# Edge pass of a GNN + FFN kernel: small norm chains on GpSimd, segment marks from memory, a fifth row-made chunk

## Chip, cores and metric

The kernel runs on one core of one Trainium2 chip. The metric is the device time of one execution in microseconds, lower is better. TensorE (PE), VectorE (DVE), ScalarE (ACT), GpSimd (POOL) and SyncE (SP) each work through their own instruction queue in order; what one needs of another it waits for by a semaphore.

## What is computed

A graph layer over 50,000 nodes of 768 features (12 heads of 64) and 25,000 edges sorted by target, then a feed-forward layer. The part that the change touches, cut from the reference:

```python
hv  = layernorm(x).reshape(n, 12, 64)
ft  = einsum('nhd,od->nho', hv, W)
a1  = sum(ft * attn_l, -1);  a2 = sum(ft * attn_r, -1)
e   = leaky_relu(a1[src] + a2[dst], 0.2)
m   = segment_max(e, dst);   w = exp(e - m[dst])
alpha = w / segment_sum(w, dst)[dst]
agg = segment_sum(alpha * ft[src], dst)
out = relu(agg + einsum('nhd,od->nho', hv, W_res))
```

After it `x + out` goes through a second layernorm and `gelu(. @ W1 + b1) @ W2 + b2`, in a node pass of 392 tiles that the change leaves alone.

## The kernel before

**Tiling.** The edge pass takes the edges in 196 chunks of 128 (one edge per partition). Seven chunks are a group (`G`, 28 groups); fourteen are a body (`BODY`), the unit of the loop `turns(...)` that each engine runs for itself. An engine's turn `c` does the stages of different chunks: a stage with lag `L` works on chunk `c - L`. GpSimd runs some five turns ahead of VectorE: its power for a group's target norms stands at turn 7g+23 of its own loop (L604 to L610), where VectorE's use of it stands at turn 7g+18 (L1348 to L1362).

**GpSimd** (L602 to L653). Per chunk: the gather of source rows (L619), the gather of target rows through `gather_targets` (L597) and a scatter of row numbers to `row_scratch` (L638), each an indirect DMA behind a `settle` (a no-op that keeps its place). Per group: two powers to the minus one half over seven columns, `r_d` for the target norms (L610) and `r_s` for the source norms (L653; L647 for group 0).

**VectorE** (from L1172). Per chunk: `bn_stats`/`bn_aggr` of the gathered source rows (L1105, L1108), the one-hot mask (L1312), the message product `ft * alpha` (L1255, two inputs from SBUF) and the sum row with its mean correction (L1237). Per group: the small norm operations `ve_s` (L1190, variance + eps, then GpSimd's power) and `nm_s` (L1202); `ve_d` (L1246), then after GpSimd's power `nmd` (L1354) and the edge scores `e_col` (L1356 to L1362); `same_x` (L1183), the marks "same target as the edge before" spread over heads; the copies of the transposed scores and marks `e_row`, `same_r` (L1318, L1319); `pen_r` (L1367); four scans (L1369 to L1385); softmax factors (L1325 to L1329).

**Target scores** are made in two ways. In ten of fourteen chunks PE transposes the target rows too and takes the products (L910, L947, L973), and VectorE copies 13 columns (L1219). In the four chunks of `OFF_PE` they are row-made: ScalarE takes the mean of the target rows (L763), VectorE multiplies them by a row of weights (L1345) and reduces per head (L1336). ScalarE also normalizes the source rows with `nm_s` and `r_s` (L742) and squares the target rows with an accumulator into `q_d` (L787).

**PE** per group transposes `e_col` and `same_x` into one bank (L934, L935), and later the weights and totals (L940, L941). **SP** loads the targets of a group over all partitions (L512) and stores each chunk's sum row to `agg_scratch` (L518), in the order of its loop.

```python
w = (i - 7) // G % 2
dve.wait_ge(s_ag, G * (gv + 1))
V.tensor_scalar(ve_s[:, w, :], mvs[:, w, :, 1], EPS, None, ALU.add).then_inc(s_ve, 1)
```

```python
pool.wait_ge(s_ved, gd + 1)
settle(pool)
pool.tensor_tensor(r_d[:, w, :], ve_d[:, w, :], half[:, 0:G], ALU.pow).then_inc(s_rpd, 1)
```

Of the kernel before, what the change touches and what calls it, by code (L numbers as in the profile page):

```python
# [8 lines left out]
D = 768  # L9
HEADS = 12  # L10
# [4 lines left out]
P = 128  # L15
# [11 lines left out]
G = 7  # L27
# [32 lines left out]
OFF_PE = (1, 6, 8, 13)  # L60
# [76 lines left out]
def gnn_ffn_kernel(nc, x, x_cols, edges, dst_rows, dst_next, dst_prev, dst_ends, chunk_base, sel_heads,  # L137
# [9 lines left out]
    with ExitStack() as ctx:  # L147
# [8 lines left out]
        row_d = nc.dram_tensor("row_scratch", [NP, RW], i32).ap()  # L156
        cls_d = nc.dram_tensor("cls_scratch", [NCLS, D], f32).ap()
# [88 lines left out]
        same_x = sb("same_x", [P, 2, HG])  # L246
# [85 lines left out]
        cnt_ps = ps[0:EH, 5, 0:2]  # L332
        a2_ps = ps[:, 6, 2 * P:2 * P + HM]
# [32 lines left out]
        s_dsl = sem("s_dsl")  # L366
# [101 lines left out]
        def _(sp):  # L468
# [12 lines left out]

            sp.dma_start(ident[:], eye).then_inc(l_const, 16)
# [110 lines left out]
        def _(pool):  # L593
# [4 lines left out]

            pool.wait_ge(l_edges, 16 * 3)
            for b in turns(pool, NB, 2):  # L600
                for i in range(BODY):
# [43 lines left out]
                    if isinstance(b, int) and c == G + 1:  # L645
                        pool.wait_ge(s_ve, 1)
                        pool.tensor_tensor(r_s[:, 0, :], ve_s[:, 0, :], half[:, 0:G], ALU.pow).then_inc(s_rp, 1)  # L647
                    gp = 2 * b + (i - 11) // G
                    if k == 11 % G and exists(gp, NG) and not (isinstance(gp, int) and gp == 0):
                        w = (i - 11) // G % 2  # L650
                        pool.wait_ge(s_ve, gp + 1)
                        settle(pool)
                        pool.tensor_tensor(r_s[:, w, :], ve_s[:, w, :], half[:, 0:G], ALU.pow).then_inc(s_rp, 1)  # L653
# [74 lines left out]
        def _(act):  # L728
# [5 lines left out]
            for b in turns(act, NB, 2):  # L734
                for i in range(BODY):
# [14 lines left out]
                    if exists(ct, EC):  # L750
# [5 lines left out]
                        if (i - L_TR) % BODY in OFF_PE:  # L756
# [822 lines left out]
```

## Time and profile before

| | us |
|---|---|
| median of three runs | 2668.76 (2667.09 to 2670.31) |
| profiled execution: its time | 2669.66 |
| its span, first to last instruction | 2667.8 |
| busy: PE, VectorE, ScalarE, GpSimd | 2562.7, 2472.9, 2364.0, 2142.9 |
| edge pass, about | 0 to 950 |
| node pass, about | 1000 to 2650 |

A row of instruction groups gives line, engine, operation, output and inputs with shapes, the number of instructions, their busy time, the mean of one in ns, and the idle time of the engine just in front of them with what ended it. "issue" means that the profile shows nothing that the engine waited for. A timeline row gives start, duration and, in brackets, idle time in front. Matmul ends are modelled, and spans on GpSimd are rough.

### The profile page before, as it was taken

What the parts mean: (1) busy time and instruction counts of PE and PEld (TensorE: products, weight loads), DVE (VectorE), ACT (ScalarE), POOL (GpSimd) and SP (SyncE); (2) the same over time, 40 slices, a digit from 0 to 9 for tenths busy, and PEclk for the clock granted to TensorE, in tenths of its full rate; (3) what the DMA queues carried; (4) which work ended last, traced back from release to release, by engine and by line L of the source; (5) the groups of instructions that cost most, each with busy time, mean ns of one, the idle gap of its engine ahead of it and who ended that gap; (6) DMA issues with size and microseconds to landing.
All of it is one profiled execution on the core that took longest, in us unless ns stands there. A gap on an engine that the chain in (4) does not pass through costs nothing. (4 is left out here: it accounts for less than half of the span.)

```text
span 2667.8 us, 67341 instructions
## 1 busy us (share of the span) xinstructions
PE 2562.7 (96%) x20334; PEld 2315.5 (87%) x20334; DVE 2472.9 (93%) x4949; ACT 2364.0 (89%) x4748; POOL 2142.9 (80%) x2029
## 2 busy tenths in 40 slices
PE   5899999999999967999999999999999999999998
PEld 4777777777777846999999999999999999999997
DVE  6799999999999886999999999999999999999996
ACT  4999999999999955999999999999999999999993
POOL 6777777877777618888888888888888888888882
PEclk9999999999999987999999999999999999999999
DMA  8788888878888567999999999999999999999983
GB/s 313 225 268 268 266 267 264 271 265 265 265 269 266 172 210 276 353 345 336 333 333 326 323 326 324 321 319 316 310 326 316 316 318 314 313 310 311 313 311 120
DMA packets 254176, 777.85 MB, mean 292 GB/s; under 512 B 77185, under 2 KB 85165, under 8 KB 253837
## 3 DMA queue, kind: packets, MB, share of 16 engines
q1 hardware_dynamic: 184190, 563.88, 59.7%
q0 software_dynamic: 69312, 210.37, 25.5%
q8 instruction: 121, 1.98, 0.3%
q14 instruction: 121, 0.99, 0.1%
q10 hardware_dynamic: 432, 0.62, 0.1%
HBM read 638.86 MB, written 236.65 MB: 328 GB/s over the span
## 5 line engine op out<-in xcount | busy, mean ns | idle before, releaser
L1057 PE MATMUL ps<-wr_bd,arena 128*128 128x128 f32 x4704 | 593.9, 277 | 13.9 <-DVE arena L1457 13.9
L1057 PEld LDWEIGHTS ps<-wr_bd,arena 128*128 128x128 f32 x4704 | 563.8, 193 | 15.3 <-issue 15.2
L723 POOL DMA_INDIRECT arena<-agg_scratch,nrow x392 | 439.1, 1120 | 77.7 <-issue 66.0
L664 POOL TENSOR_SCALAR arena<-csr_neg,mv,r_n 128x768 f32<-128x768 f32 x392 | 387.2, 988 | 51.1 <-PE ps L893 37.9
L1452 DVE SCALAR_TENSOR_TENSOR ps<-ps,r_n,arena 128x768 f32<-128x768 f32 x392 | 399.1, 1018 | 12.5 <-DMA arena<-agg_scratch,nrow 10.8
L843 ACT ACTIVATE t_hi<-ps 128x768 fp32r<-128x768 f32 x392 | 314.5, 802 | 93.9 <-PE ps L893 93.8
L1457 DVE SCALAR_TENSOR_TENSOR arena<-ps,arena 128x768 f32<-128x768 f32 x392 | 375.5, 958 | 13.4
L852 ACT ACTIVATE arena<-arena,s_st 128x768 f32<-128x768 f32 x392 | 363.8, 928 | 25.0 <-DVE arena L1457 25.0
L713 POOL TENSOR_SCALAR arena<-arena,nm_n,r_n 128x768 f32<-128x768 f32 x392 | 383.2, 978 | 2.5 <-issue 1.7
L1464 DVE TENSOR_TENSOR t_lo<-ps,t_hi 128x768 fp32r<-128x768 f32 x392 | 373.6, 953 | 12.6 <-ACT t_hi L843 12.4
L811 ACT ACTIVATE arena<-arena,mv 128x768 f32<-128x768 f32 x392 | 367.8, 938 | 12.8
L1440 DVE TENSOR_TENSOR arena<-arena,ps 128x768 f32<-128x768 f32 x392 | 369.9, 944 | 6.8 <-PE ps L1048 6.6
L1032 PE MATMUL ps<-t_hi,w_hi 128*96 128x256 f32 x1176 | 362.1, 308 | 0.0
L1032 PE MATMUL ps<-t_hi,w_lo 128*96 128x256 f32 x1176 | 330.6, 281 | 0.0
L893 PE MATMUL ps<-ident,arena 128*128 128x128 f32 x2352 | 323.3, 274 | 7.2 <-POOL arena L713 6.5
L1032 PE MATMUL ps<-t_lo,w_hi 128*96 128x256 f32 x1176 | 329.8, 280 | 0.0
L804 ACT ACTIVATE arena<-arena 128x768 f32<-128x768 f32 x392 | 326.2, 832 | 2.6 <-DMA nrow<-row_scratch 1.9
L658 POOL TENSOR_TENSOR r_n<-ve_n,half 128x4 f32<-128x4 f32 x200 | 208.3, 1041 | 119.1 <-DVE ve_n L1162 118.3
L919 PE MATMUL ps<-wgv,arena 128*128 128x130 f32 x2352 | 299.1, 277 | 0.0
L919 PEld LDWEIGHTS ps<-wgv,arena 128*128 128x128 f32 x2352 | 282.1, 193 | 0.2 <-issue 0.2
L893 PEld LDWEIGHTS ps<-ident,arena 128*128 128x128 f32 x2352 | 270.7, 142 | 9.0 <-POOL arena L713 8.2
L910 PE MATMUL ps<-ident,arena 128*128 128x128 f32 x2016 | 260.4, 277 | 16.1 <-DVE arena L1223 13.4
(226 smaller groups left out, 6171.5 us busy)
## 6 DMA issues: line engine op xcount, KB each, us to landing
arena<-in_x SPq DMA_DIRECT2D x196, 768.0 KB
arena<-in_x_cols SPq DMA_DIRECT2D x392, 384.0 KB, 5.2
out<-arena SPq DMA_DIRECT2D x195, 768.0 KB, 5.7
agg_scratch<-agg_ring SPq DMA_DIRECT2D x196, 384.0 KB, 3.6
dst_all<-in_dst_rows SPq DMA_DIRECT2D x28, 256.0 KB
arena<-agg_scratch,nrow POOLq DMA_INDIRECT x392
arena<-in_x,e_slot POOLq DMA_INDIRECT x364, 4.8
dst_all<-in_dst_rows SPq DMA_DIRECT2D x28, 192.0 KB
```

The lines of the kernel that those rows point to most:

```text
L664: pool.tensor_scalar(g_ring[:, g, :].rearrange("p (c f) -> p c f", f=P), csr_neg[:, None, :].to_broadcast([P, NC, P]), mv1[:, w, 2 * (v % ...
L713: pool.tensor_scalar(n2[:, v % 2, :], y_ring[:, v, :], nm_n[:, w, k:k + 1], r_n[:, w, PAIR + k:PAIR + k + 1], ALU.add, ALU.mult).then_inc( ...
L723: pool.indirect_dma_start(g_ring[:, g, :], None, agg_d, bass.IndirectOffsetOnAxis(nrow[:, v, 3:4], 0), bounds_check=EP - 1, oob_is_err=Fal ...
L811: nc.scalar.activation(junk[:, 0, :], x_ring[:, v, :], ACT.Square, bias=mv1[:, w, 2 * k:2 * k + 1], scale=-1.0, accum_out=q_st[:, w, k:k + ...
L893: last = nc.tensor.transpose(dst[:, c * P:(c + 1) * P], src[:, c * P:(c + 1) * P], ident[:])
L919: last = nc.tensor.matmul(ft_ps[:, n // 3, n % 3, :], both_t[:, v, n * P:(n + 1) * P], wgv[:, n, :], start=True, stop=True)
L1032: last = nc.tensor.matmul(ps[0:HID, 6 + v, 0:PAIR * P], w[:, i, :], h[:, i, :], start=(i == 0 and n == 0), stop=(i == NC - 1 and n == 2))
L1057: last = nc.tensor.matmul(res_ps(b, tr)[:, i * P:(i + 1) * P], xt_ring[:, g, i * P:(i + 1) * P], wr_bd[:], start=True, stop=True)
L1440: V.tensor_tensor(y_ring[:, v, :], y_ring[:, v, :], down_ps(b, to), ALU.add).then_inc(s_o, 1)
L1452: V.scalar_tensor_tensor(z, z, r_n[:, w, k:k + 1], g_ring[:, g, :], ALU.mult, ALU.add).then_inc(s_z1, 1)
L1457: V.scalar_tensor_tensor(y_ring[:, v, :], z, 0.0, x_ring[:, v, :], ALU.max, ALU.add, accum_out=s_st[:, w5, k:k + 1]).then_inc(s_y, 1)
L1464: V.tensor_tensor(t2_lo[:, v, :, f], pair(0).rearrange("p (c n) -> p c n", c=NC), t2_hi[:, v, :, f].bitcast(f32), ALU.subtract).then_inc(s ...
```

## The change

1. Five small operations per group move from VectorE to GpSimd, around the powers there: `ve_s`, the negated mean and its product with `r_s` (one VectorE operation before, two on GpSimd), `ve_d` and `nmd`. GpSimd now waits for `s_ag` and `s_sqd` itself, and each dependent step within a chain waits for the step before.
2. The segment marks are transposed once by PE (turn 12), kept as `same` and `(same - 1) * BIG`, written by SP to a scratch tensor with one copy per head, and loaded by SP per group straight into `same_r` and `pen_r`. `same_x`, its transpose, the copy of `same_r` and the operation for `pen_r` go.
3. `OFF_PE` gets a fifth member, 11.

```diff
-OFF_PE = (1, 6, 8, 13)
+OFF_PE = (1, 6, 8, 11, 13)
+        seg_d = nc.dram_tensor("seg_scratch", [2, EC, HEADS, P], f32).ap()
+        seg_t = agg_ring[0:EH, 2, 0:4 * P].rearrange("p (k n e) -> p k n e", k=2, n=2)
+        seg_ps = ps[0:EH, 5, 2 * P:4 * P].rearrange("p (n e) -> p n e", n=2)
...
+            def load_segments(g):
+                for k, rows in enumerate((same_r, pen_r)):
+                    sp.dma_start(rows[:, 0:P], seg_d[k].rearrange("(g c) h e -> g (c h) e", c=G)[ds(g, 1)].rearrange("g r e -> (g r) e"))                        .then_inc(d_seg, 16)
...
+                    if isinstance(b, int) and b == 1 and i == 0:
+                        sp.wait_ge(s_idx, 2)
+                        for k in range(2):
+                            for n in range(2):
+                                sp.dma_start(seg_d[k, n * EH:(n + 1) * EH], seg_t[:, k, n, :][:, None, :].to_broadcast([EH, HEADS, P]))                                    .then_inc(d_seg, 16)
+                        sp.wait_ge(d_seg, 16 * 4)
+                        load_segments(0)
+                    gs_ = 2 * b + (i - 21) // G + 1
+                    if (i - 21) % G == 0 and exists(gs_, NG) and not (isinstance(gs_, int) and gs_ < 1):
+                        sp.wait_ge(s_tot, gs_)
+                        load_segments(gs_)
...
+            def source_scale(w, gp):
+                pool.wait_ge(s_ag, G * (gp + 1))
+                at_least(pool, s_norm, G * (gp - 1))
+                settle(pool)
+                pool.tensor_scalar(ve_s[:, w, :], mvs[:, w, :, 1], EPS, None, ALU.add).then_inc(s_ve, 1)
+                pool.tensor_scalar(nm_s[:, w, :], mvs[:, w, :, 0], -1.0, None, ALU.mult).then_inc(s_ve, 1)
+                pool.wait_ge(s_ve, 2 * gp + 2)
+                settle(pool)
+                pool.tensor_tensor(r_s[:, w, :], ve_s[:, w, :], half[:, 0:G], ALU.pow).then_inc(s_rp, 1)
+                pool.wait_ge(s_rp, gp + 1)
+                settle(pool)
+                pool.tensor_tensor(nm_s[:, w, :], nm_s[:, w, :], r_s[:, w, :], ALU.mult).then_inc(s_nm, 1)
...
+                        pool.wait_ge(s_sqd, G * (gd + 1))
+                        settle(pool)
+                        pool.tensor_scalar(ve_d[:, w, :], q_d[:, w, :], 1.0 / D, EPS, ALU.mult, ALU.add).then_inc(s_ved, 1)
                         pool.wait_ge(s_ved, gd + 1)
+                        at_least(pool, s_e, 2 * (gd - 1))
                         settle(pool)
                         pool.tensor_tensor(r_d[:, w, :], ve_d[:, w, :], half[:, 0:G], ALU.pow).then_inc(s_rpd, 1)
+                        pool.wait_ge(s_rpd, gd + 1)
+                        at_least(pool, s_eo, G * (gd - 1))
+                        settle(pool)
+                        pool.tensor_tensor(nmd[:, w, :], a2_all[:, w, :, HEADS], r_d[:, w, :], ALU.mult).then_inc(s_nmd, 1)
...
-                        pool.tensor_tensor(r_s[:, 0, :], ve_s[:, 0, :], half[:, 0:G], ALU.pow).then_inc(s_rp, 1)
+                        source_scale(0, 0)
...
+                            at_least(act, s_nmd, 2 * b + (i - L_TR) // G - 1)
...
-                        nc.tensor.transpose(row_ps[:, 0:P], e_col[:, w, :], ident[:])
-                        nc.tensor.transpose(row_ps[:, P:2 * P], same_x[:, w, :], ident[:]).then_inc(s_ert, 1)
+                        nc.tensor.transpose(row_ps[:, 0:P], e_col[:, w, :], ident[:]).then_inc(s_ert, 1)
...
+                        for n in range(2):
+                            nc.tensor.transpose(seg_ps[:, n, :], same_f[:, n * EH:(n + 1) * EH], ident[:])
...
-                        V.tensor_copy(same_x[:, w, :].rearrange("p (g h) -> p g h", h=HEADS),
-                                      same_f[:, ds(G * gc, G)][:, :, None].to_broadcast([P, G, HEADS])).then_inc(s_dsl, 1)
...
-                        V.tensor_scalar(ve_s[:, w, :], mvs[:, w, :, 1], EPS, None, ALU.add).then_inc(s_ve, 1)
...
-                        V.scalar_tensor_tensor(nm_s[:, w, :], mvs[:, w, :, 0], -1.0, r_s[:, w, :],
-                                               ALU.mult, ALU.mult).then_inc(s_nm, 1)
...
-                        V.tensor_scalar(ve_d[:, w, :], q_d[:, w, :], 1.0 / D, EPS, ALU.mult, ALU.add).then_inc(s_ved, 1)
...
+                        V.tensor_copy(seg_t[:, 0], seg_ps)
+                        V.tensor_scalar(seg_t[:, 1], seg_ps, 1.0, BIG, ALU.subtract, ALU.mult).then_inc(s_idx, 1)
...
+                        if k == 0:
+                            at_least(dve, s_nm, 2 * b + i // G - 1)
                         source_stats(c, i, i // G, k, 2 * b + i // G)
...
-                        V.tensor_copy(same_r[:, 0:P], row_ps[:, P:2 * P]).then_inc(s_same, 1)
...
-                        V.tensor_tensor(nmd[:, w, :], a2_all[:, w, :, HEADS], r_d[:, w, :], ALU.mult).then_inc(s_nmd, 1)
...
-                        V.tensor_scalar(pen_r[:, 0:P], same_r[:, 0:P], 1.0, BIG, ALU.subtract, ALU.mult).then_inc(s_seg, 1)
-                        dve.wait_ge(s_seg, 3 * gm + 1)
+                        dve.wait_ge(d_seg, 32 * gm + 96)
```

## Rows read from the trace of the kernel before

**Rows 1.** Busy time by stretch; engine busy us (instructions), clock, DMA share, GB/s.

```profile
0.00:100.00 100.00, 61.24 (x504) 55.21 (x505) 59.75 (x180) 63.98 (x118) 71.74 (x74) 0.95 0.79 268
...
200.00:300.00 100.00, 98.22 (x787) 78.39 (x785) 95.83 (x227) 91.00 (x178) 78.79 (x71) 1.00 0.82 268
```

**Rows 2.** Waits of 200 to 800 us: us in total, times, longest.

```profile
ACT arena L742 <- DVE nm_s L1202: 27.4, 18, 1.8
...
DVE nmd L1354 <- POOL r_d L610: 0.5, 3, 0.2
```

**Rows 3.** GpSimd's groups, 162.18 to 818.60 us: busy us, mean ns, idle before, releasers.

```profile
L638 POOL DMA_INDIRECT row_scratch<-e_slot x140 | 157.9, 1128 | 44.5 <-issue 37.4 <-PE ps L910 5.9 <-DVE ve_d L1246 0.9
...
L619 POOL DMA_INDIRECT arena<-in_x,e_slot x140 | 152.4, 1088 | 46.4 <-issue 43.2 <-PE ps L963 2.6 <-ACT arena L787 0.3
...
L610 POOL TENSOR_TENSOR r_d<-ve_d,half 128x7 f32<-128x7 f32 x20 | 40.0, 2000 | 3.0 <-DVE ve_d L1246 3.0
```

**Rows 4.** GpSimd's timeline, five of the `r_d` powers: start us, us, instruction, idle before.

```profile
73.87 1.54 POOL L610 TENSOR_TENSOR r_d<-ve_d,half 128x7 f32<-128x7 f32 x1
...
467.43 1.54 POOL L610 TENSOR_TENSOR r_d<-ve_d,half 128x7 f32<-128x7 f32 x1
...
499.97 1.53 POOL L610 TENSOR_TENSOR r_d<-ve_d,half 128x7 f32<-128x7 f32 x1
...
531.71 2.08 POOL L610 TENSOR_TENSOR r_d<-ve_d,half 128x7 f32<-128x7 f32 x1 [0.16 <-DVE ve_d L1246]
...
893.78 1.55 POOL L610 TENSOR_TENSOR r_d<-ve_d,half 128x7 f32<-128x7 f32 x1
```

**Rows 5.** VectorE's groups, 195.32 to 326.51 us (four groups of chunks).

```profile
L1345 DVE SCALAR_TENSOR_TENSOR arena<-arena,a_all 128x768 f32<-128x768 f32 x8 | 8.1, 1011 | 0.0
...
L1336 DVE TENSOR_REDUCE a_all<-arena 128x12 f32<-128x768 f32 x8 | 7.6, 946 | 0.0
...
L1219 DVE COPY a_all<-ps 128x13 f32<-128x13 f32 x20 | 3.3, 166 | 0.0
...
L1367 DVE TENSOR_SCALAR pen_r<-same_r 84x128 f32<-84x128 f32 x4 | 1.3, 336 | 0.1
...
L1319 DVE COPY same_r<-ps 84x128 f32<-84x128 f32 x4 | 1.1, 272 | 0.0
...
L1183 DVE COPY same_x<-same_f 128x84 f32 x4 | 0.9, 230 | 0.0
...
L1190 DVE TENSOR_SCALAR ve_s<-mvs 128x7 f32<-128x7 f32 x4 | 0.7, 180 | 0.7 <-issue 0.7
...
L1246 DVE TENSOR_SCALAR ve_d<-q_d 128x7 f32<-128x7 f32 x4 | 0.7, 164 | 0.0
...
L1202 DVE SCALAR_TENSOR_TENSOR nm_s<-mvs,r_s 128x7 f32<-128x7 f32 x4 | 0.6, 156 | 0.0
```

**Rows 6.** DMA issues: KB each, median us to landing.

```profile
agg_scratch<-agg_ring SPq DMA_DIRECT2D x196, 384.0 KB, 3.6
```

**Rows 7.** GpSimd in the node pass (timeline) and its memset at the start.

```profile
1499.62 1.04 POOL L658 TENSOR_TENSOR r_n<-ve_n,half 128x4 f32<-128x4 f32 x1 [0.26 <-DVE ve_n L1162]
...
1500.87 0.99 POOL L664 TENSOR_SCALAR arena<-csr_neg,mv,r_n 128x768 f32<-128x768 f32 x1 [0.21 <-PE ps L893]
...
L1569 POOL MEMSET const-float32-1.0<- 128x1 f32 x1 | 0.1, 98 | 0.0
```

**Rows 8.** Timeline of VectorE and GpSimd around 400 us.

```profile
399.98 0.96 DVE L1255 TENSOR_TENSOR arena<-arena,alpha 128x768 f32<-128x768 f32 x1
...
400.24 2.08 POOL L610 TENSOR_TENSOR r_d<-ve_d,half 128x7 f32<-128x7 f32 x1 [0.18 <-DVE ve_d L1246]
```

**Rows 9.** Single lines, 130 to 850 us: duration ns min/median/max, first and last start.

```profile
L619 POOL DMA_INDIRECT arena<-in_x,e_slot x154: 965/1022/1472, 129.7 to 846.6; - x154
...
L638 POOL DMA_INDIRECT row_scratch<-e_slot x154: 1001/1012/1692, 132.3 to 849.4; - x154
...
L1255 DVE TENSOR_TENSOR arena<-arena,alpha x153: 944/952/957, 133.3 to 846.7; 128x768 f32<-128x768 f32 x153
```

More of the change, by code:

```diff
@@ L245, in gnn_ffn_kernel @@
         dst_slot = sb("dst_slot", [P, 2, G])
-        same_x = sb("same_x", [P, 2, HG])
         bn_a = sb("bn_a", [P, 2, 2, 6])
@@ L365, in gnn_ffn_kernel @@
         s_nmd = sem("s_nmd")
-        s_dsl = sem("s_dsl")
+        d_seg = sem("d_seg")
         s_norm = sem("s_norm")
@@ L645, in _ @@
                     if isinstance(b, int) and c == G + 1:
-                        pool.wait_ge(s_ve, 1)
-                        pool.tensor_tensor(r_s[:, 0, :], ve_s[:, 0, :], half[:, 0:G], ALU.pow).then_inc(s_rp, 1)
+                        source_scale(0, 0)
                     gp = 2 * b + (i - 11) // G
                     if k == 11 % G and exists(gp, NG) and not (isinstance(gp, int) and gp == 0):
[L650 to L653, printed above, removed]
+                        source_scale((i - 11) // G % 2, gp)
             def power(w, q):
@@ L1179, in _ @@
                         w = (i - 17) // G % 2
-                        at_least(dve, s_ert, gc - 1)
                         at_least(dve, s_mask, G * (gc - 1))
                         V.tensor_copy(dst_slot[:, w, :], dstbf[:, ds(G * gc, G)])
-                        V.tensor_copy(same_x[:, w, :].rearrange("p (g h) -> p g h", h=HEADS),
-                                      same_f[:, ds(G * gc, G)][:, :, None].to_broadcast([P, G, HEADS])).then_inc(s_dsl, 1)
                     gv = 2 * b + (i - 7) // G
                     if k == 0 and exists(gv, NG):
-                        w = (i - 7) // G % 2
-                        dve.wait_ge(s_ag, G * (gv + 1))
-                        V.tensor_scalar(ve_s[:, w, :], mvs[:, w, :, 1], EPS, None, ALU.add).then_inc(s_ve, 1)
                         if isinstance(gv, int) and gv == 0:
@@ L1195, in _ @@
                             V.tensor_tensor(w2_lo[:], w2_sb, w2_hi[:].bitcast(f32), ALU.subtract).then_inc(s_wgv, 1)
-                    gn = 2 * b + (i - 8) // G
-                    if k == 1 and exists(gn, NG):
-                        w = (i - 8) // G % 2
-                        dve.wait_ge(s_rp, gn + 1)
-                        at_least(dve, s_norm, G * (gn - 1))
-                        V.scalar_tensor_tensor(nm_s[:, w, :], mvs[:, w, :, 0], -1.0, r_s[:, w, :],
-                                               ALU.mult, ALU.mult).then_inc(s_nm, 1)
                     ge = 2 * b + (i + 6) // G
@@ L1242, in _ @@
                     gd = 2 * b + (i - L_VD) // G
-                    if (i - L_VD) % G == 0 and exists(gd, NG):
-                        w = (i - L_VD) // G % 2
-                        dve.wait_ge(s_sqd, G * (gd + 1))
-                        V.tensor_scalar(ve_d[:, w, :], q_d[:, w, :], 1.0 / D, EPS, ALU.mult, ALU.add).then_inc(s_ved, 1)
                     cm = c - L_MSG
@@ L1317, in _ @@
                             at_least(dve, s_esc, on_pe(b, i - L_FT + 1))
-                        V.tensor_copy(e_row[:], row_ps[:, 0:P])
-                        V.tensor_copy(same_r[:, 0:P], row_ps[:, P:2 * P]).then_inc(s_same, 1)
+                        V.tensor_copy(e_row[:], row_ps[:, 0:P]).then_inc(s_same, 1)
                     if (i - 21) % G == 0 and exists(ga, NG):
@@ L1352, in _ @@
                         dve.wait_ge(s_eft, G * (gd + 1))
-                        at_least(dve, s_eo, G * (gd - 1))
-                        V.tensor_tensor(nmd[:, w, :], a2_all[:, w, :, HEADS], r_d[:, w, :], ALU.mult).then_inc(s_nmd, 1)
                         at_least(dve, s_ert, gd - 1)
@@ L1366, in _ @@
                         dve.wait_ge(s_same, gm + 1)
-                        V.tensor_scalar(pen_r[:, 0:P], same_r[:, 0:P], 1.0, BIG, ALU.subtract, ALU.mult).then_inc(s_seg, 1)
-                        dve.wait_ge(s_seg, 3 * gm + 1)
+                        dve.wait_ge(d_seg, 32 * gm + 96)
                         V.tensor_tensor_scan(f_row[:], pen_r[:, 0:P], e_row[:], -BIG, ALU.add, ALU.max)\
                             .then_inc(s_seg, 1)
-                        dve.wait_ge(s_seg, 3 * gm + 2)
+                        dve.wait_ge(s_seg, 2 * gm + 1)
                         at_least(dve, s_wst, gm)
@@ L1374, in _ @@
                                              ALU.add, ALU.max).then_inc(s_seg, 1)
-                        dve.wait_ge(s_seg, 3 * gm + 3)
+                        dve.wait_ge(s_seg, 2 * gm + 2)
                         V.tensor_tensor(f_row[:], e_row[:], m_row[:], ALU.subtract).then_inc(s_z, 1)
```

1 line of the change is left out of this document (removed).

## The prediction

> **What bounds the kernel now.** The change touches only the edge pass, so I read that stretch alone. The busy table first: from 200 to 300 us PE, VectorE and ScalarE stand at 98, 96 and 91% and GpSimd at 79% [rows 1]. By shares GpSimd has room; the next views say otherwise. The table of waits (200 to 800 us, 18 groups of seven chunks): VectorE waits 0.5 us for GpSimd's `r_d` and, elsewhere, for nothing but its own results; ScalarE waits 27.4 us for VectorE's `nm_s` [rows 2]. So VectorE sets the pace and ScalarE follows. GpSimd's groups come third. Before each of its gathers and scatters it stands about 0.3 us, mostly for no cause that the profile knows ("issue"): 44.5 us before the 140 scatters of L638, 37.4 of it so [rows 3]. Three DMA instructions of about 1 us and three such gaps fill most of a chunk's 4.7 us, and twice in seven chunks a power of 1.5 to 2.1 us comes on top. Beyond that its one regular wait is 3.0 us in 20 groups, 0.15 us each, for VectorE's `ve_d` [rows 3].
>
> How much room is that? The order of the powers in time tells. At 467.43 and 499.97 us `r_d` started with no idle time in front of it (GpSimd was late), and the next began at 531.71 with 0.16 us of waiting. Those two groups took GpSimd 32.54 and 31.58 us, on average 32.06 [rows 4]. From the first `r_d` (73.87) to the 26th (893.78), 25 groups took 819.91 us, 32.80 each [rows 4]. GpSimd thus has about 0.74 us to spare in a group, and VectorE waits for `r_d` in that same group: there is no deeper buffer between the two.
>
> **VectorE, what goes.** Per group: `same_x` 0.230, `same_r` 0.272, `pen_r` 0.336, and four operations on seven columns (`ve_s`, `nm_s`, `ve_d`, `nmd`) between 0.156 and 0.180, together 0.66; 0.18 of idle time before `ve_s` goes too: 1.68 us [rows 5]. What comes: a fifth row-made chunk in fourteen, 1.011 + 0.946 for product and reduction, less a copy of 0.166: 1.79 us per body, 0.90 per group [rows 5]. Net 0.78 us less per group: VectorE alone would take 32.02.
>
> **PE, ScalarE, SP.** PE loses six transposes, six score products and one small product per body and a transpose per group; VectorE does not wait for PE, so I count nothing. ScalarE trades three copies and a score copy for two copies and one 768-column pass with an accumulator; whatever the difference, 1.5 us per group of standing before `nm_s` covers it [rows 2]; without that cover it would lie on the path at full price. SP gets two loads of 42 KB per group behind `s_tot`. That count comes from VectorE's turn 7g+13, and the store queued behind it waits for turn 7g+14, so the wait delays nothing; scans use the marks five chunks (23 us) later, while a 384 KB store lands in 3.6 us [rows 6]. Cover gone, its landing time would stand before the first scan. Four writes of 588 KB at the start take about 9 us at 268 GB/s [rows 1]; behind them in SP's queue is the first target load, five turns later. Two transposes and two small PSUM operations there fall into a stretch in which VectorE is 60% busy [rows 1]: nothing. The new waits of VectorE (`s_nm`, two groups old) and ScalarE (`s_nmd`, likewise) are long met.
>
> **GpSimd, what comes.** Per group five operations on seven columns: `ve_s`, the negated mean and the product with `r_s`, and `ve_d` and `nmd`. All three gathers or scatters of a chunk stand behind them, and behind `r_d` VectorE's `e_col`. In front of them are waits for `s_ag` and `s_sqd`; the operations that waited for these on VectorE stood 0.18 us without a named cause (`ve_s`) and not at all (`ve_d`) [rows 5], and GpSimd comes later than VectorE did: zero. The trace has no such operation. From below: a memset of one column, 0.10 us, which reads nothing [rows 7]. From above: the four-column power, 1.04 [rows 7], of which much is the power itself. Between: seven columns take 1.54 [rows 4], four 1.04, so 0.167 per column and about 0.37 for none. These operations read SBUF as that power does, so I take 0.30, an estimate, near that value. Each chain gains two dependent steps within GpSimd; in the node pass the operation that follows its power so starts 0.21 us after it [rows 7]. Sum: 5 x 0.30 + 4 x 0.21 = 2.34 us.
>
> **A lock, by row and rule.** `r_d` at 400.24 took 2.08 instead of 1.54 us; it started 0.26 us into VectorE's message product (399.98 to 400.94) [rows 8]. The gathers show the same in their spread, 965 to 1472 ns, while the 153 message products lie between 944 and 957 [rows 9]: GpSimd pays, VectorE never. The Trainium skill, SBUF — State Buffer, section on the two sides of SBUF, says a VectorE instruction with two SBUF inputs and a GpSimd instruction that reads SBUF exclude each other, whichever starts first. The trace agrees for GpSimd as the second and not for VectorE as the second; were that half to hold, ten short operations per body would also hold VectorE up, by my estimate well under 1 us per body. The lock now costs about 2.2 us per group (seven source gathers and seven scatters at means of 1088 and 1128 against least values of 965 and 1001 ns, and 0.46 for `r_d`) [rows 3, 9], over nine such passes of VectorE (seven message products, two products of row-made chunks). The fifth row-made chunk is half a product more per group: 0.12 us.
>
> **Sum.** GpSimd: 32.06 + 2.34 + 0.12 = 34.52 us per group against VectorE's 32.02. GpSimd becomes the bound: it waits for nobody, and VectorE stands before `e_col`. 25 groups x 34.52 = 863.0, which is 43.1 more than 819.91. Before the first `r_d`, for which VectorE already waited, three more chains: about 3 us. After the 26th VectorE paces again and gains about 2 us in the last two groups. Together +44 on the profiled execution's 2669.66: 2713.8; that execution is 0.9 above the median of the runs, so 2713.
>
> The Trainium skill, GPSIMD Engine Reference, section Performance versus the Vector engine, gives 4497 ns for 2048 columns; at that rate seven cost 0.015 us (an estimate from that page) and the sum would be some 38 us lower, 2675.
>
> **Rivals.** (a) GpSimd keeps up and VectorE paces: 25 x 0.78 = 20 us less, 2649. Its place is GpSimd's queue between two `r_d`. It needs 34.52 to fall to 32.02: operations at 0.10 give back 1.0, and the lock would have to give back another 1.5 of its 2.2, which it can, since where GpSimd's starts fall depends on phase. For it: one late group took GpSimd only 31.58 [rows 4]. Against it: two losses must shrink together. It decides where GpSimd's group passes 32.02. (b) Nothing to see: operations at 0.10 and a lock cost smaller by 0.7: 32.8 per group, 2670. (c) Operations at the price of the four-column power, 1.04: 3.7 us more in each of 25 groups and 6 in the first chains, 2811. (d) The marks arrive late and each scan waits: 3.6 us on 28 groups would be 100 us, but only if the loads were queued five chunks late; nothing in SP's order does that.
>
> **Chances.** The forecast, GpSimd pacing with operations between 0.10 and 0.38: 0.72, and its own range is 2686 (0.10) to 2735 (0.38 and a lock 0.45 per group dearer). (a) 0.16, (b) 0.08, (c) and (d) together 0.04. The range holds (b) and much between (a) and (b): 2655 to 2745. What a measurement of this kernel can tell from no change is about 0.2% (5 us; the runs before span 3.2). Faster 0.16, within it 0.08, slower 0.76.
>
> **Signs.** Right, if `r_d` stand about 34.5 us apart, GpSimd shows no idle time before them, VectorE stands about 2.5 us per group before `e_col` with `r_d` as releaser, and the five operations measure 0.2 to 0.4. Wrong, if the powers again wait for VectorE or ScalarE (then (a)), if the small operations are far from 0.30, or if VectorE stands before the scans (then (d)). One more message-product stretch should show in GpSimd's mean durations.

## The result and the profile after

The changed kernel takes 2744.13 us (median of four runs, 2741.94 to 2746.37) against 2669.53 us before (four runs, 2667.09 to 2673.12): ratio 1.0278 [1.0261, 1.0296], slower by 74.6 us. 44 us were forecast (2713), and the measured median lies 1 us inside the upper end of the range, 2745. The profiled execution of after took 2742.53 us with a span of 2740.7, 72.9 more than the span before.

**Where the time went.** GpSimd's timeline of after, four of its `r_d` powers (start us, us, instruction, idle before):

```profile
76.60 1.51 POOL L644 TENSOR_TENSOR r_d<-ve_d,half 128x7 f32<-128x7 f32 x1
...
361.00 1.52 POOL L644 TENSOR_TENSOR r_d<-ve_d,half 128x7 f32<-128x7 f32 x1 [0.24 <-POOL ve_d L640]
...
397.61 1.52 POOL L644 TENSOR_TENSOR r_d<-ve_d,half 128x7 f32<-128x7 f32 x1 [0.23 <-POOL ve_d L640]
...
966.12 1.52 POOL L644 TENSOR_TENSOR r_d<-ve_d,half 128x7 f32<-128x7 f32 x1 [0.17 <-POOL ve_d L640]
```

The first and the 26th stand 889.52 us apart, 35.58 per group (36.6 and 34.5 in turn for most of the way), where [rows 4] gave 819.91 and 32.80: +69.6 us. The first `r_d` comes 2.7 later. From the 26th to the end it takes 1774.6 us, against 1774.0 before. 2.7 + 69.6 + 0.6 = 72.9, the whole difference of the spans: all of it arises in the steady groups of the edge pass and in the start.

**Who paces.** The busy table of after, 200 to 300 us (columns as in [rows 1]):

```profile
200.00:300.00 100.00, 89.78 (x689) 70.95 (x681) 87.81 (x188) 85.61 (x165) 76.96 (x79) 0.98 0.79 246
```

VectorE's groups of after, 200 to 860 us (columns as in [rows 5]):

```profile
L1373 DVE TENSOR_TENSOR e_col<-a_all,r_d 128x84 f32<-128x84 f32 x18 | 4.6, 258 | 49.7 <-ACT arena L809 30.6 <-POOL r_d L644 19.1
```

Against [rows 1] PE, VectorE and ScalarE lost 8, 8 and 5 points of busy share, and GpSimd 2: its busy share does not show that it now paces. VectorE stands 49.7 us in 18 groups, 2.76 each, before `e_col`, where it had waited 0.5 us in all for GpSimd before [rows 2]. The row puts 30.6 us of this on a ScalarE copy, and here it misleads, as the timelines of VectorE and ScalarE around 399 us show:

```profile
398.40 0.83 ACT L809 ACTIVATE arena<-ps 128x780 f32<-128x780 f32 x1
...
399.35 0.25 DVE L1373 TENSOR_TENSOR e_col<-a_all,r_d 128x84 f32<-128x84 f32 x1 [3.40 <-ACT arena L809]
```

`r_d` of that group ran from 397.61 to 399.13, and `e_col` began 0.22 us later. The copy named belongs to another chunk; the last one that `e_col` needs had ended at 386.87, 12 us before. In every group of this stretch `e_col` begins 0.22 to 0.23 us after its `r_d` has ended, so all 49.7 us are waits for GpSimd.

GpSimd's groups of after, 200 to 860 us (busy us, mean ns, idle before, releasers), to set beside [rows 3]:

```profile
L657 POOL DMA_INDIRECT arena<-in_x,e_slot x130 | 151.5, 1165 | 52.1 <-issue 39.7 <-PE ps L945 9.1 <-ACT arena L822 2.4
L676 POOL DMA_INDIRECT row_scratch<-e_slot x130 | 143.3, 1102 | 39.6 <-issue 34.1 <-PE ps L996 4.3 <-ACT arena L822 0.6
L614 POOL DMA_INDIRECT arena<-in_x,e_slot x130 | 135.6, 1043 | 41.1 <-issue 36.9 <-PE ps L996 2.4 <-ACT arena L776 1.8
L644 POOL TENSOR_TENSOR r_d<-ve_d,half 128x7 f32<-128x7 f32 x19 | 28.9, 1520 | 4.4 <-POOL ve_d L640 4.4
L624 POOL TENSOR_TENSOR r_s<-ve_s,half 128x7 f32<-128x7 f32 x18 | 27.4, 1520 | 2.7
L620 POOL TENSOR_SCALAR ve_s<-mvs 128x7 f32<-128x7 f32 x18 | 5.7, 317 | 0.4
L648 POOL TENSOR_TENSOR nmd<-a_all,r_d 128x7 f32<-128x7 f32 x18 | 5.3, 292 | 4.0 <-POOL r_d L644 4.0
L621 POOL TENSOR_SCALAR nm_s<-mvs 128x7 f32<-128x7 f32 x18 | 4.5, 252 | 1.4
L640 POOL TENSOR_SCALAR ve_d<-q_d 128x7 f32<-128x7 f32 x19 | 4.1, 216 | 1.4
L627 POOL TENSOR_TENSOR nm_s<-nm_s,r_s 128x7 f32<-128x7 f32 x19 | 4.1, 216 | 2.7
```

L657 is the source gather (L619 before), L676 the scatter (L638), L614 the target gather (L597). The five new operations take 216 to 317 ns, 1.28 us per group together. The powers now wait only for GpSimd's own step in front of them. GpSimd works through its list without a stop for VectorE, and that list has become the group's time.

**The account of a group.** From such rows I take a group of each kernel apart (200 to 860 us). *Stretch* is what the three DMA instructions take beyond their least durations, 7 times the sum of (mean less least), with 965, 942 and 1001 ns as least for source gather, target gather and scatter: here 7 x (200 + 101 + 101) = 2.81 us. *Powers* is what the two powers take beyond 1.512 us each, *idle* is the idle time before all of GpSimd's instructions, *small* the operations of the chains. *Group* is 7 x 660 us over the number of chunks counted in the stretch, so it is good to some 0.25 us; the spacing of the `r_d` is the finer measure:

| us per group | group | stretch | powers | idle | small |
|---|---|---|---|---|---|
| before | 32.77 | 1.95 | 0.54 | 6.98 | 0 |
| after | 35.54 | 2.81 | 0.02 | 8.07 | 1.28 |

+0.86, -0.52, +1.09 and +1.28 make 2.71 of the 2.77 that the group grew. GpSimd's timeline of after shows the idle part, in both chains:

```profile
411.98 0.31 POOL L620 TENSOR_SCALAR ve_s<-mvs 128x7 f32<-128x7 f32 x1
412.37 0.25 POOL L621 TENSOR_SCALAR nm_s<-mvs 128x7 f32<-128x7 f32 x1
412.78 1.52 POOL L624 TENSOR_TENSOR r_s<-ve_s,half 128x7 f32<-128x7 f32 x1
414.44 0.21 POOL L627 TENSOR_TENSOR nm_s<-nm_s,r_s 128x7 f32<-128x7 f32 x1
415.34 1.11 POOL L657 DMA_INDIRECT arena<-in_x,e_slot  x1 [0.69 <-issue]
...
431.64 0.21 POOL L640 TENSOR_SCALAR ve_d<-q_d 128x7 f32<-128x7 f32 x1
432.09 1.52 POOL L644 TENSOR_TENSOR r_d<-ve_d,half 128x7 f32<-128x7 f32 x1 [0.24 <-POOL ve_d L640]
433.83 0.21 POOL L648 TENSOR_TENSOR nmd<-a_all,r_d 128x7 f32<-128x7 f32 x1 [0.22 <-POOL r_d L644]
434.73 1.08 POOL L657 DMA_INDIRECT arena<-in_x,e_slot  x1 [0.69 <-issue]
```

Each dependent step costs 0.2 us, as forecast. What was not: the gather behind a short operation starts 0.58 to 0.69 us after its end; behind a power, in the kernel before, it was nearly always 0.18 to 0.20. In both cases that is twice in a group.

### The profile page after: what moved, and what is told of

Same layout as the page of the kernel before. It is cut to its first block and busy times, and to the rows that moved or that the text cites. A ratio compares the mean times of both kernels' runs of the same rounds, so it can differ in the third digit from the quotient of the medians.

```text
span 2740.7 us, 66968 instructions
## 1 busy us (share of the span) xinstructions
PE 2550.6 (93%) x20028; PEld 2299.2 (84%) x20028; DVE 2471.8 (90%) x4769; ACT 2368.3 (86%) x4748; POOL 2190.5 (80%) x2169
## 5 line engine op out<-in xcount | busy, mean ns | idle before, releaser
L928 PE MATMUL ps<-ident,arena 128*128 128x128 f32 x2352 | 321.9, 273 | 7.6 <-POOL arena L747 6.8
L776 ACT ACTIVATE arena<-arena,nm_s,r_s 128x768 f32<-128x768 f32 x196 | 200.4, 1023 | 83.6 <-POOL nm_s L627 83.6
```

What stands on the lines that cost most here:

```text
L928: last = nc.tensor.transpose(dst[:, c * P:(c + 1) * P], src[:, c * P:(c + 1) * P], ident[:])
```

## The experiments

Each kernel was timed against the kernel before on the same chip (its medians there 2670.7 to 2671.5 us). Theory 1 is the prediction's: GpSimd's list of work sets the group, and the chains and the lock lengthen it. The lock is what the prediction calls it: VectorE's passes with two SBUF operands (the message product and the product of a row-made chunk) hold GpSimd's instructions up.

**Four row-made chunks instead of five**, with chains and marks as in after:

```diff
-OFF_PE = (1, 6, 8, 11, 13)
+OFF_PE = (1, 6, 8, 13)
```

> The changed kernel with four row-made chunks again, chains on GpSimd and marks from memory kept. Theory (GpSimd's instruction stream paces the edge pass, 35.5 us per group): only 0.12 us of stalls per group go, 2741 us (2733 to 2746), and VectorE stands longer before e_col. Rival 1 (VectorE paces; what was added to it is what costs): 0.90 us per group in 28 groups, 2719. Rival 2 (the marks from memory are what costs): no change, 2744, but then chains_dve stays high as well.

Measured: 2716.49, 1.0176 [1.0159, 1.0193]. A miss: one chunk in fourteen is worth 27.6 us, not a few. GpSimd's three DMA lines, 200 to 860 us:

```profile
L614 POOL DMA_INDIRECT arena<-in_x,e_slot x134 | 143.4, 1070 | 42.3 <-issue 31.4 <-ACT arena L776 5.8 <-PE ps L996 5.1
L657 POOL DMA_INDIRECT arena<-in_x,e_slot x134 | 141.4, 1055 | 54.2 <-issue 40.7 <-PE ps L945 11.1 <-ACT arena L822 2.4
L676 POOL DMA_INDIRECT row_scratch<-e_slot x134 | 138.9, 1037 | 40.8 <-issue 34.1 <-PE ps L996 5.8 <-PE ps L945 0.6
```

Stretch falls from 2.81 to 7 x (90 + 128 + 36) = 1.78 us; idle (8.08) and small operations (1.27) stay. The group falls by 0.97 (35.58 to 34.61 by the spacing of the `r_d`), so it is stretch alone. The time also lies near rival 1's 2719, but VectorE does not pace here. It still stands 2.1 us per group for `r_d`, as its table of waits shows (us in total, times, longest):

```profile
DVE e_col L1373 <- POOL r_d L644: 40.1, 19, 3.4
```

Half a product per group lasts 0.5 us and can hold GpSimd no longer than that by itself; where the rest comes from is counted below, behind the run without the message product.

**Both chains back on VectorE**, five chunks and marks kept:

```diff
-            def source_scale(w, gp):
...
-                        source_scale((i - 11) // G % 2, gp)
+                        w = (i - 11) // G % 2
+                        pool.wait_ge(s_ve, gp + 1)
+                        settle(pool)
+                        pool.tensor_tensor(r_s[:, w, :], ve_s[:, w, :], half[:, 0:G], ALU.pow).then_inc(s_rp, 1)
...
-                        pool.tensor_scalar(ve_d[:, w, :], q_d[:, w, :], 1.0 / D, EPS, ALU.mult, ALU.add).then_inc(s_ved, 1)
...
+                        V.tensor_scalar(ve_s[:, w, :], mvs[:, w, :, 1], EPS, None, ALU.add).then_inc(s_ve, 1)
...
+                        V.scalar_tensor_tensor(nm_s[:, w, :], mvs[:, w, :, 0], -1.0, r_s[:, w, :],
+                                               ALU.mult, ALU.mult).then_inc(s_nm, 1)
...
+                        V.tensor_scalar(ve_d[:, w, :], q_d[:, w, :], 1.0 / D, EPS, ALU.mult, ALU.add).then_inc(s_ved, 1)
...
+                        V.tensor_tensor(nmd[:, w, :], a2_all[:, w, :, HEADS], r_d[:, w, :], ALU.mult).then_inc(s_nmd, 1)
```

> The changed kernel with both small chains back on VectorE (as before the change), five row-made chunks and marks from memory kept. Theory: GpSimd is back at about 32.2 us per group and VectorE paces with 32.80 - 0.84 + 0.90 = 32.86: 2671 us (2666 to 2680). Rival 1 (the fifth row-made chunk costs): about 2694 or more. Rival 2 (marks from memory cost): stays above 2700.

Measured: 2677.13, 1.0025 [1.0012, 1.0037]. As expected; rivals 1 and 2 fall. The chains on GpSimd are worth 67.0 of the 74.6 us (2744.13 - 2677.13).

**Only one of the chains on GpSimd.** The edit above for the target chain alone (the source chain stays on GpSimd):

```diff
-                        pool.tensor_scalar(ve_d[:, w, :], q_d[:, w, :], 1.0 / D, EPS, ALU.mult, ALU.add).then_inc(s_ved, 1)
...
-                        pool.tensor_tensor(nmd[:, w, :], a2_all[:, w, :, HEADS], r_d[:, w, :], ALU.mult).then_inc(s_nmd, 1)
...
+                        V.tensor_scalar(ve_d[:, w, :], q_d[:, w, :], 1.0 / D, EPS, ALU.mult, ALU.add).then_inc(s_ved, 1)
```

> Only the source chain (s_ag, ve_s, mean, r_s, nm_s) on GpSimd; the target chain back on VectorE; five row-made chunks and marks kept. Theory: about half of what both chains add to GpSimd's 32.2 us per group, 0.79 for three operations, 0.4 for two handshakes and 0.45 for the later start of the gather behind the short operation: 33.8 per group, 2669 + 25 x 1.0 = 2695 (2685 to 2710). Rival (the target chain alone does it, as it is the one that VectorE waits for): 2675 or less.

Measured: 2713.99, 1.0167 [1.0150, 1.0184], above the range. And the other way round, the source chain back on VectorE and the target chain left on GpSimd:

```diff
-            def source_scale(w, gp):
...
+                        V.tensor_scalar(ve_s[:, w, :], mvs[:, w, :, 1], EPS, None, ALU.add).then_inc(s_ve, 1)
...
+                        V.scalar_tensor_tensor(nm_s[:, w, :], mvs[:, w, :, 0], -1.0, r_s[:, w, :],
+                                               ALU.mult, ALU.mult).then_inc(s_nm, 1)
```

> Only the target chain (s_sqd, ve_d, r_d, nmd) on GpSimd, the source chain back on VectorE; five row-made chunks and marks kept. Theory: 0.51 for two operations, 0.45 for two handshakes, 0.45 for the later gather, on GpSimd's 33.0 us per group: 34.2, 2703 us (2693 to 2715). Rival (the chains cost only together): 2685 or less.

Measured: 2687.66, 1.0059 [1.0042, 1.0076], below the range and next to the rival. So the target chain alone costs 10.5 us over no chain, the source chain alone 36.9, both 67.0: they don't add up. In the account:

| us per group | group | stretch | powers | idle | small |
|---|---|---|---|---|---|
| no chain on GpSimd | 33.08 | 1.89 | 0.57 | 7.28 | 0 |
| target chain | 33.64 | 2.29 | 0.16 | 7.28 | 0.60 |
| source chain | 34.39 | 2.86 | 0.03 | 7.18 | 1.03 |
| both (after) | 35.54 | 2.81 | 0.02 | 8.07 | 1.28 |

The small operations cost what they take. Stretch and powers change with every shift of GpSimd's starts, by up to 1 us, and only the kernel with both chains pays more idle time.

**The lock, taken away.** The message product reads two operands from SBUF; here two `bn_stats` passes over the same rows, with one operand each, stand in its place. The messages stay unweighted, so the softmax weights don't reach the output:

```diff
-                        V.tensor_tensor(msg, msg,
-                                        per_head(alpha[:, w, j * HEADS:(j + 1) * HEADS])[:, :, :, None]
-                                        .to_broadcast([P, NC, HC, DH]), ALU.mult).then_inc(s_msg, 1)
+                        for h in range(2):
+                            last = V.bn_stats(bn_m[:, v, h, :], ft_ring[:, v, 3 * h:3 * h + 3, :].rearrange("p a b -> p (a b)"))
+                        last.then_inc(s_msg, 1)
```

> The changed kernel without the message product: in its place two bn_stats passes over the same chunk of ft_ring (one SBUF input each, some 0.1 us longer together), so the messages are left unweighted. Theory (VectorE's passes with two SBUF inputs hold GpSimd's instructions up): of 2.8 us of stretched gathers and scatters per group about 2 go, 33.5 us per group, 2744 - 50 = 2694 us (2684 to 2720), gathers close to their least durations although VectorE is busier. Rival (the stretch belongs to the gathers themselves or to any work of VectorE): 2738 or more.

Measured: 2702.13, 1.0120 [1.0100, 1.0140], 42.0 us below after, although VectorE's passes are longer (2 x 553 against 951 ns). GpSimd's DMA lines and VectorE's new passes:

```profile
L658 POOL DMA_INDIRECT arena<-in_x,e_slot x136 | 143.8, 1057 | 54.3 <-issue 45.4 <-PE ps L997 5.8 <-PE ps L946 3.1
L677 POOL DMA_INDIRECT row_scratch<-e_slot x137 | 139.9, 1022 | 41.7 <-issue 35.7 <-PE ps L997 5.5 <-PE ps L946 0.6
L615 POOL DMA_INDIRECT arena<-in_x,e_slot x136 | 136.1, 1001 | 43.0 <-issue 40.7 <-PE ps L997 2.1 <-ACT arena L823 0.3
...
L1272 DVE BATCH_NORM_STATS2 bn_m<-arena 128x6 f32<-128x390 f32 x272 | 139.2, 553 | 0.0
```

Stretch falls to 1.20 us; the group falls by 1.65 (to 33.89), of which stretch is 1.61. 25 x 1.65 = 41 us: the whole gain. So 1.6 of the 2.8 us of stretch go with the message product's second SBUF operand. By itself this run leaves a rival: the new passes also shift the phase, and phase alone changes stretch. The traces close it. In after, VectorE's pass first, then the GpSimd instruction that started while it ran:

```profile
215.25 0.95 DVE L1271 TENSOR_TENSOR arena<-arena,alpha 128x768 f32<-128x768 f32 x1
...
215.44 1.65 POOL L676 DMA_INDIRECT row_scratch<-e_slot  x1 [0.31 <-issue]
...
228.19 1.01 DVE L1364 SCALAR_TENSOR_TENSOR arena<-arena,a_all 128x768 f32<-128x768 f32 x1
...
228.29 1.77 POOL L657 DMA_INDIRECT arena<-in_x,e_slot  x1 [0.30 <-issue]
```

The message product ends at 216.20 and the scatter 0.89 us later; the row-made product ends at 229.20 and the gather 0.86 us later. A held instruction thus ends its least duration, less some 0.1 us, after the pass that it met. Over the traces of the eleven kernels here that have both the message product and GpSimd's powers (200 to 860 us), by where a DMA instruction starts (only those directly behind another DMA instruction; some steps of 0.1 us are left out):

| start, counted from the start of the nearest two-operand pass, us | instructions | mean stretch, us |
|---|---|---|
| 0.8 to 0.2 before | 682 | 0.01 |
| 0.1 before to 0.1 after | 166 | 0.39, from 0 to 0.90 |
| 0.1 to 0.2 after | 72 | 0.70 |
| 0.3 to 0.4 after | 185 | 0.48 |
| 0.5 to 0.6 after | 157 | 0.30 |
| 0.7 to 0.8 after | 83 | 0.09 |
| 0.8 to 0.9 after | 28 | 0.01 |

One pass costs GpSimd between nothing and 0.9 us, by where in it the instruction starts. In after, 102 of 390 instructions end in this way behind a pass; they hold 43.2 of 52.4 us of stretch, 29.4 behind message products (1.58 us per group, as much as went without them) and 13.9 behind row-made products. With four row-made chunks it is 19.9 and 0.2 us, in 72 of 402. What stays without the message product is for the most part, 13.2 of 24.5 us, behind the row-made products. The powers follow the same rule: before, 18 of 21 `r_d` started 0.24 to 0.25 us into a message product and took 2.08 us, as in [rows 8]; in after none does, hence 1.52.

The other side of it, in after (duration ns min/median/max, 130 to 900 us):

```profile
L1271 DVE TENSOR_TENSOR arena<-arena,alpha x151: 944/951/978, 133.3 to 898.4; 128x768 f32<-128x768 f32 x151
```

As before [rows 9], VectorE's product is never longer than its median by more than some 30 ns, now with five more GpSimd operations per group, and VectorE does not stand idle in front of one either (0.0 us in all before the 130 of 200 to 860 us). The Trainium skill, SBUF — State Buffer, section "SBUF: two separate sides", says that whichever of the two starts first holds the shared ports and the other waits for the whole instruction. These runs agree for GpSimd as the one that waits and show nothing of VectorE waiting.

**The same with the marks alone** (messages unweighted, four chunks, chains on VectorE); the edit is the one above and that of the next run together.

> The same replacement in the kernel with the marks alone (which took 2678 us with VectorE waiting for r_d in every group). Theory (there GpSimd paces through these stalls, 3.6 us per group): GpSimd falls to about 31, VectorE paces with 31.96 + 0.5 to 0.9, r_d waits for ve_d again, 2662 us (2652 to 2674). Rival (the marks' loads cost): 2678 or more, up to 2690 as VectorE does more.

Measured: 2718.38, 1.0182 [1.0164, 1.0200], a miss by 56 us, and no test of the lock. Its table of waits, 200 to 860 us:

```profile
DVE ve_s L1205 <- issue: 40.5, 9, 5.2
POOL r_s L671 <- DVE ve_s L1205: 39.4, 16, 4.7
```

Once per body VectorE stands 4 to 5 us at the same place for no cause that the profile names, and GpSimd waits for it. Of its DMA queues the second instruction queue (q14) carried 176 packets here and 120 to 122 in all the others. More instruction packets and the stops come together; that one causes the other isn't shown. What can be read: stretch is 0.89 here, the least of all these kernels.

**Marks alone**, four chunks, chains on VectorE:

```diff
-OFF_PE = (1, 6, 8, 11, 13)
+OFF_PE = (1, 6, 8, 13)
...
+                        V.tensor_scalar(ve_d[:, w, :], q_d[:, w, :], 1.0 / D, EPS, ALU.mult, ALU.add).then_inc(s_ved, 1)
```

> Only the marks from memory: both chains on VectorE, four row-made chunks. Theory: VectorE needs 31.96 us per group and GpSimd, late all the time, 32.06: about 25 x 0.74 us below before, 2651 (2647 to 2658), with r_d starting without idle time in front in many groups. If VectorE alone paced: 2646. Rival 2 (marks from memory cost): no faster than 2669.

Measured: 2678.19, 1.0030 [1.0019, 1.0042]. A miss, and the most telling one: VectorE does 0.84 us less per group (`same_x`, `same_r`, `pen_r` [rows 5]), and the kernel is 7.5 us slower. GpSimd's groups, 200 to 860 us:

```profile
L655 POOL DMA_INDIRECT row_scratch<-e_slot x140 | 182.5, 1304 | 42.7 <-issue 36.6 <-DVE ve_d L1260 3.0 <-PE ps L978 3.0
L614 POOL DMA_INDIRECT arena<-in_x,e_slot x139 | 152.8, 1100 | 42.4 <-issue 33.5 <-PE ps L927 5.8 <-DVE ve_d L1260 3.0
L636 POOL DMA_INDIRECT arena<-in_x,e_slot x139 | 138.3, 995 | 37.8 <-issue 28.0 <-PE ps L978 5.2 <-PE ps L927 4.6
L670 POOL TENSOR_TENSOR r_s<-ve_s,half 128x7 f32<-128x7 f32 x20 | 33.9, 1693 | 0.3
L627 POOL TENSOR_TENSOR r_d<-ve_d,half 128x7 f32<-128x7 f32 x20 | 30.8, 1538 | 0.1
```

VectorE's wait for it, from the table of waits of the same stretch:

```profile
DVE nmd L1369 <- POOL r_d L627: 16.0, 20, 1.4
```

`r_d` no longer waits for `ve_d` (0.1 us in 20 groups; 3.0 before [rows 3]), and VectorE waits for `r_d` in every group: GpSimd paces, at 33.2 us, without a chain on it. Stretch is 7 x (303 + 158 + 30) = 3.44 against 1.95. Against before, a group has 0.8 us less idle time and 0.3 less in the powers, and 1.5 more stretch. In the same count as above, 109 of 417 instructions meet a message product here, 0.56 us each, where before 79 of 422 met a pass, 0.40 us each: the starts have moved to the front of the product. The idle time that I had read as room went into that.

**Fewer row-made chunks**, from marks alone and from the kernel before: fewer two-operand passes, so less stretch by theory 1; the rival was that only the places where the passes fall count.

```diff
-OFF_PE = (1, 6, 8, 13)
+OFF_PE = (1, 6, 11)
```

> The marks from memory, both chains on VectorE, three row-made chunks (1, 6, 11). VectorE would need 31.06 us per group. Theory (GpSimd paces through its stalls; a row-made product less per body takes 0.5 to 1.0 us of them per group off, as between five and four): 32.2 to 32.7 per group against 33.2 with four, 2653 to 2666 us. Rival 1 (PE, with one more chunk of transposed target rows, paces): 2678 or more. Rival 2 (the stalls depend on phase alone): anywhere from 2650 to 2690, without relation to the number of products.

Measured (three chunks, marks): 2688.37, 1.0065 [1.0051, 1.0079].

```diff
-OFF_PE = (1, 6, 8, 13)
+OFF_PE = (1, 8)
```

> As marks3 with two row-made chunks (1, 8). VectorE would need 30.2 us per group. Theory: another 0.5 to 1.0 us of stalls per group off, down to GpSimd's 31.5 to 32: 2640 to 2655. Rival 1 (PE paces): more than marks3. Rival 2 (phase alone): no order between the two.

Measured (two chunks, marks): 2677.60, 1.0027 [1.0018, 1.0036].

```diff
-OFF_PE = (1, 6, 8, 13)
+OFF_PE = (1, 6, 11)
```

> The kernel before with three row-made chunks in place of four and nothing else. VectorE would need 31.9 us per group, as much as in the kernel with marks alone and four. Theory: GpSimd paces, with a product less per body: 32.2 to 33.2 per group, 2655 to 2678 us. If VectorE alone paced: 2646. Rival (PE paces): 2678 or more.

Measured (three chunks, otherwise the kernel before): 2700.53, 1.0113 [1.0098, 1.0129]. Three misses. With marks, five, four, three and two chunks give 2677, 2678, 2688 and 2678 us: no order. But these three times are no test of the lock alone. VectorE's waits, with three and with two chunks and marks (200 to 860 us):

```profile
DVE a_all L1233 <- PE ps L988: 29.9, 38, 1.4
...
DVE a_all L1233 <- PE ps L988: 35.7, 30, 1.4
```

VectorE stands 1.4 to 1.8 us per group for the score products of PE (28.0 us in the kernel with three chunks and no other change), where before and with the marks alone it stands for them not at all, and it waits for `r_d` no more than 3.5 us in all. So rival 1, PE, is in these times, and with three chunks it fits them (2688 and 2701, against 2678 or more). What the three can show is the stretch: 1.65, 3.19 and 1.88 us per group in the order of the runs. The scatter with two chunks and marks, the fewest passes of all:

```profile
L655 POOL DMA_INDIRECT row_scratch<-e_slot x140 | 180.1, 1286 | 42.7 <-issue 33.8 <-DVE ve_d L1260 5.5 <-PE ps L927 3.4
```

It is stretched as in marks alone with four: 89 of 420 instructions meet a pass, 0.63 us each. The number of passes is not what decides. That theory falls, and for the stretch rival 2, phase, stands: what counts is where in a pass an instruction starts.

**One more short operation on GpSimd behind each chain**, its result unused:

```diff
+                pool.tensor_tensor(dup[:, 0, :], half[:, 0:G], r_s[:, w, :], ALU.mult)
...
+                        pool.tensor_tensor(dup[:, 1, :], half[:, 0:G], r_d[:, w, :], ALU.mult)
```

> The changed kernel with one more short GpSimd operation (seven columns, no dependents) behind each chain. In the changed kernel the gather behind a chain starts 0.6 to 0.7 us after the last short operation, where it starts 0.2 us after a power. Theory 1 (a gather needs some 0.9 us from the start of what is in front of it, and a short operation leaves that uncovered): the added operation lies in that gap, 2744 to 2748. Theory 2 (each operation costs its own length): 0.5 us per group, 2757.

Measured: 2746.30, 1.0285 [1.0268, 1.0302], 2 us above after, for 2 x 0.21 us in 28 groups (12 us). GpSimd's timeline:

```profile
417.54 0.21 POOL L628 TENSOR_TENSOR nm_s<-nm_s,r_s 128x7 f32<-128x7 f32 x1
417.71 0.21 POOL L629 TENSOR_TENSOR dup<-half,r_s 128x7 f32<-128x7 f32 x1
418.46 1.11 POOL L660 DMA_INDIRECT arena<-in_x,e_slot  x1 [0.54 <-issue]
```

From the start of `nm_s` to that of the gather it is 0.92 us here and 0.90 in after: the added operation lies in the gap. The gap is the price of having short operations last in front of a DMA, not of their number.

**Both roots on ScalarE.** From marks alone: GpSimd loses its powers, ScalarE takes exp(-0.5 ln(var + eps)) for both.

```diff
-                        pool.tensor_tensor(r_d[:, w, :], ve_d[:, w, :], half[:, 0:G], ALU.pow).then_inc(s_rpd, 1)
...
+                            nc.scalar.activation(ve_d[:, w, :], q_d[:, w, :], ACT.Ln, bias=eps_c[:], scale=1.0 / D).then_inc(s_ved, 1)
+                            act.wait_ge(s_ved, gq + 1)
+                            at_least(act, s_nmd, gq - 1)
+                            nc.scalar.activation(r_d[:, w, :], ve_d[:, w, :], ACT.Exp, scale=-0.5).then_inc(s_rpd, 1)
```

> A version from the experiments: marks from memory, four row-made chunks, and no power on GpSimd in the edge pass: ScalarE makes both reciprocal roots as exp(-0.5 ln(variance + eps)), two short operations for each, VectorE keeps nm_s, nmd and e_col and loses ve_s and ve_d. Theory (GpSimd's instruction stream is what stands in the way): GpSimd falls to 26.7 us per group and 2 to 3.5 of stretch, below VectorE's 31.4, so VectorE paces: 2669 - 25 x 1.3 = 2636 us (2628 to 2650), gathers waiting for PE again. Rival 1 (PE or ScalarE, about 30 busy and now 1 us more, paces at 32.5 or above): 2660 or more. Rival 2 (ScalarE reloads its tables at each change between ln and exp, 1.28 us each as the table loads in the trace, four per group): ScalarE at 35 or more, 2720 or more.

Measured: 2802.44, 1.0493 [1.0479, 1.0507], a miss; rival 2 is met. ScalarE's groups, 200 to 860 us:

```profile
L805 ACT ACT_TABLE_LOAD x18 | 23.1, 1283 | 0.3
L807 ACT ACT_TABLE_LOAD x18 | 23.1, 1283 | 0.3
L796 ACT ACT_TABLE_LOAD x17 | 21.8, 1283 | 1.7
L799 ACT ACT_TABLE_LOAD x17 | 21.8, 1283 | 0.3
```

GpSimd's longest waits, from the table of waits of the same stretch:

```profile
POOL row_scratch L650 <- PE ps L980: 96.2, 43, 3.6
POOL arena L631 <- PE ps L929: 73.0, 53, 1.8
```

Four table loads of 1.283 us stand in every group, 5.1 us. The Trainium skill, ScalarE: Activation LUTs, section "Table sets: the hidden batching unit", has one set that holds both functions, one load for a logarithm and an exponential. This run does not agree: each of the four operations has its own load. Of use here is the second view: this is what GpSimd looks like when it does not pace, with 169 us of waits for PE where the longest of after's rows have 9.1 and 4.3.

No version beat the kernel before.

## Why the prediction was right, and where it fell short

**The mechanism held.** GpSimd became the bound, VectorE stands before `e_col` (2.76 us per group; about 2.5 forecast), `r_d` waits for nothing but GpSimd's own step, the small operations lie between 0.2 and 0.4 us, and the scans wait for nothing, so the marks come in time. Moving the chains back gives 67 of 74.6 us back. Rival (a), GpSimd keeps up, needed the lock to shrink; it grew. Rival (c), operations at 1.04 us, fell with their mean of 0.26 us. That is also far above the 0.015 us worked out from GPSIMD Engine Reference of the Trainium skill, section Performance versus the Vector engine: by that rate almost all of a seven-column operation's time is fixed, but no run here varies the columns.

**The size was 30 us short.** The sum gave 34.52 us per group, measured were 35.58. The run with four row-made chunks splits the difference of 1.06, as its `r_d` stand 34.61 us apart:

- **The step that failed is the price of the fifth chunk.** It was forecast at 0.12 us and measured 0.97 (34.61 to 35.58), +0.85. The prediction took the cost per two-operand pass as constant (2.2 us over nine passes) and added half a pass; the stretch it brought is 1.03 us, because the starts of GpSimd's instructions moved within all passes, the message products too (1.06 to 1.58 us per group).
- All else: 32.06 + 2.34 = 34.40 forecast, 34.61 measured, only +0.21. That is luck, for its errors cancel. The five operations took 1.27 in place of 1.50: -0.23. The lock (stretch and powers together) fell from 2.49 to 1.79, most of it by the power `r_d`, which no longer starts inside a message product: -0.70, where nothing was forecast. The four handshakes came as forecast, 0.2 each (the row that gave 0.21 names PE as what ended the idle time; the value was right all the same), but a gather behind a short operation starts 0.4 to 0.5 us later, twice in a group, which the list of steps did not have. Idle time so grew by 1.10 over a group that held 0.16 of waiting for `ve_d` before [rows 3], by 1.26 against 0.84: +0.42.
- What is left, +0.72, falls to the free group of 32.06 from two late ones [rows 4]. It counts on 0.74 us to spare, of which the trace shows 0.16 as waiting; that accounts for 0.58, and 0.14 stays unassigned. Without a chain on GpSimd and with VectorE relieved, GpSimd's group was 33.2, not 32.06. Two late groups were too few to tell how fast GpSimd can go; idle time in front of its DMA instructions was not room.

25 x 1.06 = 26.5 us of the miss are these; the tail adds 2.6 (2 us of gain forecast, 0.6 lost); the start came as forecast, 2.7 against 3. That the result still lies inside the range, by 1 us, is luck as well.

**What stays open.** What sets the phase. The traces show that stretch of 3.4 us in one kernel and 1.8 in another follows from where in VectorE's passes GpSimd's instructions start, but not why a given kernel settles at those starts, so the stretch of a new kernel can't be forecast from this. No schedule that keeps the two apart was tried. Nor was the cause of VectorE's stop in the run with 176 instruction packets found.

## What to carry to other kernels

Before work is moved to an engine that looks idle, see what ends its idle time: GpSimd at 79% waited for VectorE only 0.16 us in a group of 32.8, and with VectorE relieved it set the pace at once. A lock between two engines has no price per pass that can be added up; take it as a range, read from the timeline where in the pass the other engine's instructions start, and measure it by exchanging the two-operand pass for one with a single operand. A short operation last in front of a DMA leaves a gap, in which one more was free; putting such operations between others instead was not tried.

## What the runs showed of the hardware

A seven-column operation on GpSimd takes 0.21 to 0.32 us, a dependent one starts some 0.2 us after the one before it, and an indirect DMA instruction starts about 0.9 us after the start of a short operation in front of it, with one more short operation between them at no cost (0.92 against 0.90). Short operations are held too: with the source chain alone on GpSimd all 19 `ve_s` of 200 to 860 us started inside a message product and ended 0.12 us after it, 568 ns on average against 317 in after.

A GpSimd instruction that starts while VectorE runs a pass with two SBUF operands is held until the pass ends (stretch of 0.70 us for a start 0.1 to 0.2 us into it, 0.09 for one at 0.7 to 0.8); one that starts 0.2 us or more before the pass is not held (0.01), and VectorE's product isn't either (944 to 978 ns).
